# An attention and mixture-of-experts block: half of the second batch routed through slots of one expert, its attention gate folded into the output weights

## The reference

```python
mod = (silu(c) @ wmod).reshape(2, 6, 1, 256)
sa, ca, ga, sb, cb, gb = (mod[:, i] for i in range(6))
ga, gb = (2 * (g >= 0) - 1) * maximum(abs(g), 0.25)     # for each of the two
h = layernorm(x) * (1 + ca) + sa
x = x + ga * attention(h, wq, bq, wkv, bkv, wo)          # 16 heads of 128, causal, out @ wo
h = layernorm(x) * (1 + cb) + sb
logits = h @ gate_w.T                                    # 8 experts
top_vals, top_idx = top_k(logits, 2)
w = softmax(top_vals)
y = sum over the 2 chosen experts of w * (expert_w[e] @ h + expert_b[e])
x = x + gb * y
```

## Time and profile before

| what | value |
|---|---|
| median of 3 runs | 909.89 us (908.25 to 910.55) |
| the profiled execution, its own time | 914.3 us |
| its span, first to last instruction | 912.1 us |
| PE, DVE, ACT, POOL busy | 96%, 83%, 58%, 35% of the span |
| mean granted clock of PE | 0.994 of full speed |
| moved by DMA | 36.12 MB |

### The profile page before, as it was taken

The page is one execution under the profiler, slowest core; times in us unless marked ns, Lnnn a source line. Parts: engine busy times, 40 slices in busy tenths (PEclk is TensorE's granted clock), DMA queues, the critical chain, the costliest instruction groups (busy, mean ns, idle before and its releaser), DMA issues.

```text
span 912.1 us, 16758 instructions
## 1 busy us (share of the span) xinstructions
PE 877.0 (96%) x5337; PEld 769.0 (84%) x5337; DVE 761.5 (83%) x1725; ACT 532.2 (58%) x1223; POOL 321.4 (35%) x395
## 2 busy tenths in 40 slices
PE   5899999999999999999999999999999999898996
PEld 4788888888888888888888998888888888787774
DVE  5777888888888888878788888888889897678798
ACT  4487666666666666663766666666666665444321
POOL 3464222222222222141624444444322225417685
PEclk9999999999999999999999999999999999899999
DMA  7000400000000000300000000000000004342122
GB/s 242 7 12 13 145 13 13 12 12 12 12 12 12 12 12 13 105 12 1 16 9 13 13 13 13 12 13 13 12 13 13 13 13 141 116 166 96 57 81 82
DMA packets 31845, 36.12 MB, mean 40 GB/s; under 512 B 2506, under 2 KB 29428, under 8 KB 31604
## 3 DMA queue, kind: packets, MB, share of 16 engines
q1 hardware_dynamic: 30180, 31.08, 10.5%
q0 software_dynamic: 1536, 4.20, 1.4%
q10 hardware_dynamic: 64, 0.02, 0.0%
HBM read 28.08 MB, written 10.22 MB: 42 GB/s over the span
## 4 chain that ended last, share of the span: by engine, by line
PE 85%; DVE 8%; issue 2%; ACT 2%; DMA 1%; another core or an unknown queue 0%; POOL 0%; SPq 0%; DVEq 0%; ACTq 0%; POOLq 0%
PE ps_t L898 13%; PE ps_s L787 8%; PE ps_s L791 8%; PE ps_s L788 8%; PE ps_o L779 7%; PE ps_o L783 7%; PE ps_o L780 7%; PE ps_m L787 3%; PE ps_m L791 3%; PE ps_m L788 3%; PE ps_m L779 3%; PE ps_m L783 3%; PE ps_m L780 3%; PE ps_o L908 2%; ACT probs L1283 1%
## 5 line engine op out<-in xcount | busy, mean ns | idle before, releaser
L1233 ACT ACTIVATE pt_hi<-ps_t 128x512 fp32r<-128x512 f32 (+2 forms) x320 | 170.9, 534 | 130.1 <-PE ps_t L898 122.2
L1283 ACT ACTIVATE probs<-ps_s,neg_max 128x128 f32<-128x128 f32 (+7 forms) x256 | 189.9, 742 | 79.2 <-DVE neg_max L1636 76.4
L1645 DVE TENSOR_TENSOR pt_lo<-ps_t,pt_hi 128x512 fp32r<-128x512 f32 (+2 forms) x320 | 192.1, 601 | 16.0 <-ACT pt_hi L1233 12.2
L1636 DVE TENSOR_REDUCE neg_max<-ps_s 128x1 f32<-128x128 f32 (+7 forms) x256 | 192.3, 751 | 3.7
L898 PE MATMUL ps_t<-ident,probs 128*128 128x128 f32 x1152 | 189.0, 273 | 0.9 <-DVE pt_lo L1645 0.9
L591 POOL TENSOR_TENSOR q_lo<-raw,q_hi 128x512 fp32r<-128x512 f32 x60 | 77.4, 1290 | 318.4 <-ACT q_hi L1233 318.4
L898 PEld LDWEIGHTS ps_t<-ident,probs 128*128 128x128 f32 x1152 | 142.1, 141 | 20.8 <-DVE pt_lo L1645 4.9
L787 PE MATMUL ps_s<-k_hi,q_hi 128*128 128x512 f32 (+2 forms) x354 | 148.6, 420 | 3.8 <-ACT probs L1283 3.8
L1683 DVE SCALAR_TENSOR_TENSOR acc<-ps_m,rsum,acc 128x256 f32<-128x256 f32 x256 | 111.3, 476 | 17.6 <-PE ps_m L791 16.8
L1630 DVE TENSOR_TENSOR ps_s<-ps_s,mask 128x128 f32<-128x128 f32 x256 | 75.4, 295 | 59.1 <-PE ps_s L791 51.9
L791 PE MATMUL ps_s<-k_hi,q_lo 128*128 128x512 f32 (+2 forms) x354 | 123.4, 349 | 0.0
(11 more groups left out here) (244 smaller groups left out, 1704.7 us busy)
## 6 DMA issues: line engine op xcount, KB each, us to landing
wq_raw<-in_L_attn_wq_dram SPq DMA_DIRECT2D x32, 128.0 KB, 2.3
wo_raw<-in_L_attn_wo_dram SPq DMA_DIRECT2D x32, 128.0 KB
slot_out_dram<-y_slot SPq DMA_DIRECT2D x23, 128.0 KB, 1.7
slot_rows<-slot_rows_dram SPq DMA_DIRECT2D x2, 1280.0 KB, 10.7
wkv_raw<-in_L_attn_wkv_dram SPq DMA_DIRECT2D x2, 1024.0 KB, 6.7
x_again<-in_L_attn_x_dram SPq DMA_DIRECT2D x2, 1024.0 KB, 5.9
we_raw<-in_L_ffn_expert_w_dram SPq DMA_DIRECT2D x1, 2048.0 KB, 8.3
acc<-in_L_attn_x_dram SPq DMA_DIRECT2D x2, 512.0 KB, 4.5
```

The lines of the kernel that those rows point to most:

```text
L1233: return nc.scalar.activation(dst, src, ACT.Copy, scale=scale)
L1283: nc.scalar.activation(probs[par][:, prob_offset(i):prob_offset(i) + w], ps_s[:, i % 2, col:col + w], ACT.Exp, bias=neg_max[:, par, i:i + ...
L1636: nc.vector.tensor_reduce(neg_max[:, par, i:i + 1], ps_s[:, i % 2, col:col + w], AXIS_X, ALU.max, negate=True).then_inc(max_set, 1)
L1645: nc.vector.tensor_tensor(pt_lo[:, q % PT, lo:CH], ps_t[:, q % 2, lo:CH], pt_hi[:, q % PT, lo:CH].bitcast(F32), ALU.subtract).then_inc(pt_ ...
```

## The change

The second batch's first four tiles ("near") are now routed too, into 15 slots of their own; its last four ("late") stay dense. Core of the diff, by subject.

Sizes and order:

```diff
-SLOTS = 2 * T // P + EXPERTS - 1
+HALF = NT // 2
+SLOTS = FREE * NT + EXPERTS - 1
+SLOTS1 = FREE * HALF + EXPERTS - 1
+ALL_SLOTS = SLOTS + SLOTS1
-SLOT_OUT = 3
+SLOT_OUT = 4
+GATHERS = 4
+ROWS = ["ga1", "ga0", "gb0", "sb0", "cb0", "sb1", "cb1", "gb1"]
+SIDE = ([("rows", 0, HEADS - 1, 10, 0)]
+        + [("rows", 1, 0, q, v) for q, v in ((2, 1), (3, 2), (10, 3), (11, 4))]
...
+        + [("rows", 1, HEADS - 1, q, v) for q, v in ((2, 5), (3, 6), (10, 7))])
```

The second batch's `acc` begins as x, and its gate multiplies `wo` (POOL's 16 residual instructions go):

```diff
+                    sp.dma_start(slot_dram1, x.rearrange("b t e -> (b t) e")[0:SLOTS1 * P, :]).then_inc(slots_filled, 16)
+                    sp.wait_ge(ht_mm[1], NC * KE)
+                    sp.dma_start(acc[:, NT:2 * NT, :], x_tiles[:, NT:2 * NT, :]).then_inc(x1_sum_in, 16)
...
-            def cut_wo(n, par):
+            def cut_wo(n, par, b):
                 pool.wait_ge(wo_in, (n + 1) * 16)
+                if b == 1:
+                    if n == HEADS:
+                        pool.wait_ge(side_set, side_count("rows", ROWS.index("ga1")))
+                    pool.tensor_tensor(wo_raw[:, :], wo_raw[:, :], gate_row1[:, :], ALU.mult).then_inc(wo_scaled, 1)
+                    pool.wait_ge(wo_scaled, n - HEADS + 1)
                 if not (isinstance(n, int) and n < 2):
                     pool.wait_ge(y_mm, n * 4 - 4)
```

POOL in the frames: rows for the second batch are spread in frame 14, ahead of that frame's scatters; in frame 15 the bias tables:

```diff
+                if b == 1 and l + 2 == HEADS:
+                    pool.wait_ge(q_mm, NC * B * HEADS)
+                    pool.wait_ge(wo_cut, B * HEADS)
+                    spread_columns(("sb1", "cb1", "gb1"))
                 if b == 1 and l in SCATTER_FRAMES:
...
                 if b == 1 and l + 1 == HEADS:
-                    pool.wait_ge(q_mm, NC * B * HEADS)
-                    spread_columns(spread1, 1, (MOD_GA, MOD_GB))
+                    bias_tables()
+                    tables_again()
```

DVE in the last frame, and the slots; the bias comes from one more matmul (2 rows: high and low plane), and `slot_finish` is now in ACT's program instead of DVE's:

```diff
+                    if b + 1 == B and l + 1 == HEADS and q in (9, 10):
+                        statistics(q - 9)
+                        if q == 10:
+                            bias_low()
...
+                nc.tensor.matmul(bank, bias_ones[:, :], bias_planes[0:FREE, bass.ds(e, 1), :].rearrange("p x o -> p (x o)"),
+                                 start=True, stop=False)
...
+            def slot_finish(s):
+                act.wait_ge(slot_mm, s + 1)
+                if s >= SLOT_OUT:
+                    act.wait_ge(y_stored[s % SLOT_OUT], 16 * (s // SLOT_OUT))
+                nc.scalar.activation(y_slot[:, s % SLOT_OUT, :], slot_bank(s)[:, 0:O], ACT.Copy).then_inc(slot_out, 1)
```

PE behind the last frame:

```diff
+            turn_after = {2: 0, 4: 1, 6: 2, 8: 3, 12: 4, 13: 5, 14: 6, 15: 7}
+            gate_after = {3: (0,), 5: (1,), 7: (2,), 9: (3,), 15: (4,), 16: (5, 6), 17: (7,)}
...
+            for d in range(HALF):
+                if d == 2:
+                    pe.wait_ge(n_place_set, 1)
+                    slot_e = chosen(n_expert_u, SLOTS1)
+                    for s in range(SLOTS, ALL_SLOTS):
+                        if s + 2 < ALL_SLOTS:
+                            turn_slot(s + 2)
+                        slot_product(s, slot_e[s - SLOTS])
+                for e2 in range(EXPERTS // 2):
+                    experts(d, e2)
+                    if d == 1 and e2 >= 2:
+                        turn_slot(SLOTS + e2 - 2)
```

DVE there (the counting and placing of the near tiles, `near_counts` and `near_places`, is 22 small instructions):

```diff
-            _, slot_e = nc.values_load_multi_w_load_instructions(
-                slot_expert_u[0:1, 0:SLOTS], engines=[mybir.EngineType.DVE], min_val=0, max_val=EXPERTS - 1,
-                skip_runtime_bounds_check_because="a sum of seven comparisons lies in 0 to 7")
...
+                if s == 13:
+                    near_counts()
+                if s in (15, 16, 17):
+                    near_places(s - 15)
...
+            for d in range(HALF):
+                if d == 2:
+                    slot_lower(SLOTS)
+                    slot_lower(SLOTS + 1)
+                    for s in range(SLOTS, ALL_SLOTS):
+                        if s + 2 < ALL_SLOTS:
+                            slot_lower(s + 2)
+                        i = s - SLOTS
+                        if i % 2 == 1 and i // 2 + 2 < NT:
+                            join(i // 2 + 2)
+                mix(d)
+                if d + 2 < HALF:
+                    hidden2_lo(d + 2)
+                if d == 1:
+                    join(0)
+                    join(1)
+                if d == 3:
+                    join(NT)
+                    join(NT + 1)
+            join(NT + 2)
+            join(NT + 3)
```

ACT takes `slot_finish`, the first two of a dense tile's eight results (`mix_first`), and in the second slots `weigh_first(i // 2 + 2)` at every even slot i. POOL:

```diff
+            for m in range(HALF):
+                scatter_again(m)
+            for j in range(NT):
+                gather(j)
+                if j == 2:
+                    finish(0)
+                if j == 5:
+                    finish(1)
+            for j in range(NT, JOINS):
+                gather(j)
+            finish(2)
+            finish(3)
```

More of the change, by code:

```diff
@@ L661, in frame @@
                 if nxt:
-                    cut_wo(n + 1, 1 - par)
+                    cut_wo(n + 1, 1 - par, b)
+                if b == 1 and l == 0:
+                    pool.wait_ge(side_mm, side_count("rows", ROWS.index("gb0")))
+                    spread_columns(("sb0", "cb0"))
                 if routed is not None:
@@ L1193, in experts, with chosen @@
                 last.then_inc(moe_mm, 1)
+            def chosen(table, count):
+                return nc.values_load_multi_w_load_instructions(
+                    table[0:1, 0:count], engines=[mybir.EngineType.PE], min_val=0, max_val=EXPERTS - 1,
+                    skip_runtime_bounds_check_because="a sum of seven comparisons lies in 0 to 7")[1]
             n = B * HEADS - 1
@@ L1510, in _ @@
-            weigh_first(NT - 1)
+                if s > 0:
+                    slot_finish(s - 1)
+                if s in (3, 5, 7, 9):
+                    late_copy((s - 3) // 2)
+                if s == 10:
+                    read_logits(near, HALF)
+                if s == 12:
+                    gap_exponential(near)
+                if s in (13, 14, 15, 16):
+                    late_copy(s - 9)
+                if s == 15:
+                    read_rank()
+                if s in (17, 18):
+                    hidden2_hi(s - 17)
@@ new lines, in best_index @@
+            def best_index(c):
+                for i in range(HALF):
+                    dve.wait_ge(c["step"], i + 1)
+                    nc.vector.max_index(c["index"][:, i, :], c["top"][:, i, :], c["logits"][:, i, :]).then_inc(c["step"], 1)
+                nc.vector.tensor_tensor(c["gap"][:, :], c["top"][:, :, 1], c["top"][:, :, 0],
+                                        ALU.subtract).then_inc(c["gap_set"], 1)
+                dve.wait_ge(c["step"], 2 * HALF)
+                nc.vector.tensor_copy(c["first"][:, :, :], c["index"][:, :, 0:FREE]).then_inc(c["step"], 1)
@@ new lines, in near_counts @@
+            def near_counts():
+                c, done = near, 2 * HALF + 6
+                nc.vector.tensor_tensor(n_both[:, :, :], c["pick"][:, 0, :, :], c["pick"][:, 1, :, :],
+                                        ALU.add).then_inc(c["step"], 1)
+                nc.vector.memset(n_before[:, 0, :], 0.0)
+                dve.wait_ge(c["step"], done + 1)
+                nc.vector.tensor_copy(n_before[:, 1, :], n_both[:, 0, :]).then_inc(c["step"], 1)
+                for i in range(1, HALF):
+                    dve.wait_ge(c["step"], done + 1 + i)
+                    nc.vector.tensor_tensor(n_before[:, i + 1, :], n_before[:, i, :], n_both[:, i, :],
+                                            ALU.add).then_inc(*((c["step"], 1) if i + 1 < HALF else (n_count_set, 1)))
@@ new lines, in coefficients @@
+            def coefficients():
+                c, done = late, 2 * HALF + 6
+                dve.wait_ge(c["step"], done)
+                for f, part in enumerate((coef, coef2)):
+                    nc.vector.tensor_tensor(part[:, :, :], c["pick"][:, f, :, :],
+                                            c["weight"][:, f, :].unsqueeze(2).to_broadcast([P, HALF, EXPERTS]),
+                                            ALU.mult).then_inc(coef_step, 1)
+                dve.wait_ge(coef_step, 2)
+                nc.vector.tensor_tensor(coef[:, :, :], coef[:, :, :], coef2[:, :, :], ALU.add).then_inc(coef_set, 1)
```

915 lines of the change are left out of this document (533 added, 382 removed).

## The result

The changed kernel takes 924.5 us (924.07, 924.95 and 924.47) where the kernel before takes 909.07 (four runs from 908.21 to 910.55): a ratio of 1.0168, with a 95% interval of 1.0147 to 1.0189. A fourth run of the changed kernel, 940.06 us at a mean granted clock of 0.975 instead of 0.990, is left out of these figures. It is slower by 15 us. The forecast was 906.6 us in a range of 897 to 916 and had "slower" at 0.23; it missed the time, the range and the sign.

A forecast was written before the change was run, and what follows sets the result against it. PE was taken as the bound, so terms counted on PE or where it waits. -30.1 + 15.75 + 3.9 + 4.1 - 1.5 + 2.0 + 2.7 = -3.2, -2.9 with an added step; forecast 906.6 us, range 897 to 916.

The forecast's parts named there:

- The dense stage: Expert products of the dense tiles: four tiles at 6.47 us make 25.9 where eight made 56.0, -30.1 us.
- The second slots: Fifteen added slots of the near tiles: +15.75 us as floor, plus waits of +3.9 at their head and +4.1 for POOL's queue.
- First slots, -1.5: First slots: some 31 us of PE work without waits, DVE relieved of bias additions; -1.5 us, bounds -2 and +3.
- The floor of 1.05: Second slots: 0.93 us a slot plus half of 0.231 for the bias matmul; fifteen make +15.75 us.
- PE's hold by GpSimd's queue, +4.1: Second slots: scatters and gathers queue on POOL, `weigh_first(7)` at slot 10 holds ACT and so PE; +4.1 us, bounds 0 and 9.
- Head and end: PE waits for DVE's joins and lowering ahead of the second slots, +3.9 us; four joins instead of two at the end, +2.7.
- The clock falls: Rival: PE's new waits ahead of first product and second slots bring 1.2 GHz, up to 2.5 us each; 911.6 us, chance 0.17.
- Last frame, +2.0: Last frame: DVE's two `statistics` and `bias_low` make the first slot product later; +2.0 us, bounds 0 and +3.
- Frame 15's wait, 0: PE's 3.80 us wait ahead of its side step in frame 15 stays unchanged in length: 0, bounds +2.2 and -6.3 us.
- The wait in frame 15 vanishes: Rival: spreads no longer stand behind the scatters, so wait and slow clock go, -6.3 us; 900.3 us, chance 0.23.
- a clock under 1 in the slots: Sign in the profile after, at the slots, by which the forecast would be wrong; no size given.
- Runs of indirect DMAs hold the other engines: Rival: runs of scatters and gathers hold ACT, so PE loses about 8.5 us; 915.1 us, chance 0.18.

The follow-up runs named there:

- no_bias: The changed kernel without both kinds of bias matmul, so the sum lacks the experts' bias: 911.8 us, ratio 1.003 to the kernel before.
- bias_rows128: The changed kernel with the bias operands zero-padded from 2 to 128 rows: 914.45 us, ratio 1.0049 to the kernel before.
- no_scatter: bias_rows128 with the moves of first_slots and head_and_store, without the near tiles' eight scatters (second slots multiply other rows): ratio 0.9969 to the kernel before.
- first_slots: bias_rows128 with late tiles turned after slots 10, 12, 14, 16 and ScalarE's `late_copy` ahead of `slot_upper`: 920.7 us, ratio 1.0073.
- head_and_store: bias_rows128 with joins and last late tile's halves behind the first second slots' raisings and lowerings, second late tile's store behind eleven slot stores: 920.8 us, 1.0072.
- joins_late: The changed kernel with `join(0)` and `join(1)` moved into the second slots' loop, behind `slot_lower(s + 2)`: 931.8 us, ratio 1.0218 to the kernel before.
- bias_rows32: The changed kernel with the bias operands zero-padded from 2 to 32 rows: one run, 941.64 us at a mean clock of 0.977.
- before_again: The kernel before, unchanged, run on chip A for a second profile: 909.53 us.
- before_profile: The kernel before, unchanged, profiled once more on chip D: 914.1 us.
- after_again: The changed kernel, unchanged, run again on chip C: ratio 1.0381 to the kernel before, its profiled run 931.4 us.
- scatter_late: bias_rows128 with the moves of first_slots and head_and_store, near tiles' scatters waiting until the last first slot has left PSUM: ratio 1.0082 to the kernel before.

## Why the prediction was wrong

**The step that failed** is in "The dense stage" and "The second slots": the bias matmul, "two rows deep, taken at the price of the others since the row's step goes by columns". It costs 0.50 us in a slot, not 0.12 (against the 0.93 of the earlier trace rows; 0.48 against the 0.95 of no_bias), and 0.63 before an expert pair, not 0.23 (0.66 against the 1.36 of no_bias). 38 x 0.38 + 16 x 0.40 = 20.8 us were left out; taking them away gave 10.0 back. The matmul isn't long: a gap opens before it and another behind it. PE's timeline of before has a case that may be of the kind, the bias product of 8 rows, which I had not read:

```profile
857.25 0.48 PE L787 MATMUL ps_s<-we_hi,h_hi 128*128 128x512 f32 x1
857.57 0.40 PE L788 MATMUL ps_s<-we_lo,h_hi 128*128 128x512 f32 x1
...
858.27 0.39 PE L788 MATMUL ps_s<-we_lo,h_hi 128*128 128x512 f32 x1
858.50 0.40 PE L791 MATMUL ps_s<-we_hi,h_lo 128*128 128x512 f32 x1
858.82 0.69 PE L1177 MATMUL ps_m<-ebias,coef_t 8*128 8x256 f32 x2
```

It starts 0.32 us behind its neighbour, where the others start 0.23 apart. It proves nothing by itself: it is a float32 product and no float32r one, and 0.32 us also lie between the two products of 128 rows that follow a transposition, at 857.25 and 857.57. The Trainium skill (TensorEngine Tiling (Array Packing), Key Properties) says that a change of the tiling mode drains TensorE; the runs agree, if 2 or 32 rows of 128 count as another mode, and put the price at 0.37 us (256 columns) to 0.43 (512) for there and back. The prediction's sum had no term for it.

**First slots, -1.5.** Measured +10.3. The bias is 8.7 of it, but with 128 rows the stage is still 38.3 us long (bias_rows128), 7 over the 31 that I had counted. Of these 7, 3 are a count that my own rows contradict: PE was busy 29.20 us there before, and with the 2.7 and 2.3 that I added it is 34.2, a term of +1.6 and not -1.5. no_scatter, with 128 rows, the late tiles' moves and no hold there, takes 34.4 from the first turning to the first expert pair. The rest are waits, of which I had allowed +3. I looked for them in VectorE's small instructions; they lay in ScalarE, through which turned tiles, gates and ranks pass between a slot's two copies. The moves of first_slots alone cut these steps, and where no scatter held ScalarE (no_scatter) the products span 33.3 us instead of 37.2.

**Second slots.** The floor of 1.05 was right but for the bias (bias_rows128: 1.06). PE's hold by GpSimd's queue, +4.1, was 0 in the changed kernel, because its slots were slow enough to hide it, and 2.6 us with fast slots (a step of 3.69 instead of 1.06), at the seventh slot and by another path: not through `weigh_first(7)` at the tenth, but through SyncE's queue. The times behind the term were off too: in the changed kernel the scatters begin 35.6 us behind the first product, not 26, but the second slots begin 63.9 behind it, not 47.9, and the last of gathers 0 to 7 is issued at 880.2, ahead of the slot that needs it (889.6). Only with the head mended as well does a gather hold ScalarE (2.38 us in head_and_store).

**Head and end.** 4.08 us against 3.9, and 2.8 against 2.7: right. What was not in the sum is the 1.2 GHz behind the head: steps of 2.51 and 2.06 instead of 1.43, 1.7 us, in the size of the rival "The clock falls". The Trainium skill (TensorE: Matmul & The Clock Gate, What's actually happening) speaks of idleness as what throttles the clock; behind 4.05 us of it the trace agrees, but joins_late and bias_rows32 lost the clock behind waits of at most 0.42 us, in a stretch full of PE's short gaps at the bias matmuls. That these gaps are the cause is argued from the count above, not shown.

**Last frame, +2.0.** From the spread's turning in frame 15 to the first slot's turning it is 20.59 us instead of 19.71 (before_again), so +0.9. `bias_low` took 2.34 us, as forecast, but took the place of a wait of 1.46 that VectorE had there.

**Frame 15's wait, 0.** This term failed too. PE's wait ahead of the spread's turning is 0.52 us, where before_again has 1.83, for a spread that stood behind the scatters, and before and before_profile 3.80 and 3.92. On chip C, which has the idle times, it is 0.52 as well (after_again), and ScalarE's idle time there 1.44 instead of 4.42 (before_profile, chip D). So with the spreads ahead of the scatters the long wait is gone on either kind of chip: the rival "The wait in frame 15 vanishes" had this mechanism right. Its price of 2.5 us for the slow clock was somewhat high: 4.58 us of work at 0.54 of full speed lose 2.1. The vanished wait, and a clock under 1 in the slots, are two of the signs by which the prediction was to be known as wrong.

**The rivals.** "Runs of indirect DMAs hold the other engines" fits the chips that have the idle times (no_scatter: 7.1 us less), but in the profile of the result no such idle time stands: it had the right sign for the wrong reason. "The clock falls" came true behind both waits, some 1.3 us in the first slots and 1.7 in the second, but before_again lost some 1.7 in its slots as well. The Trainium skill's rule on GpSimd's descriptors beside VectorE (SBUF — State Buffer, SBUF: two separate sides) would have made gathers slower, if VectorE's operations here are of the kind that it names; at a mean of 979 and 945 ns they are no slower than before's 999.

## What to carry to other kernels

A float32r matmul of 2 or 32 rows among ones of 128 is not priced by its columns: pad its operands with zeros to the neighbours' rows, or keep it out of the loop, and look at the starts of PE's instructions, since the busy time hides the gaps. When a stage of one engine is sped up, list what the next engine in its chain does in each step, here ScalarE's copies and SyncE's order of stores, for that is where the gain goes. Ahead of a prediction take two profiles, and compare kernels on one chip only.

## What the runs showed of the hardware that I had not expected

A float32r matmul of 2 or 32 rows between ones of 128 costs 0.48 us with 256 columns and 0.66 with 512, one of 128 rows 0.11 and 0.23. On four of the five chips of these runs ScalarE stood idle beside runs of eight scatters with no releaser in the profile, for 1.0 to 4.4 us at a time in the frames and 6.3 to 8.3 in all beside the near tiles' scatters (none there in bias_rows32 and scatter_late); on the fifth, chip A, never, and the kernel before is 3.6 to 5.3 us faster there (909.3 against 912.9 to 914.6). TensorE can fall to 1.2 GHz for some 20 us (joins_late, 842 to 866) in a stretch where its busy time reads 16.00 of 16.00.
